# Edge stage of a graph network in ten groups of 500 edges instead of twenty pairs of tiles

## What is computed

```
n    = layernorm(x)
msg  = relu(n[src] + edge_attr @ W_e + b_e)          # 5000 x 512
aggr = segment_sum(msg, dst)                         # 10000 x 512
h    = (1 + eps) * n + aggr
h    = silu(bn(h @ W1 + b1)); h = silu(bn(h @ W2 + b2))
x    = x + h
out  = x + mixture(layernorm(x))                     # 16 experts over groups of 16 tokens
```

## Time and profile before

| | us |
|---|---|
| median of 3 runs | 2110.25 (2109.22 to 2110.86) |
| profiled execution, its time | 2105.35 |
| its span | 2103.6 |
| first stage in it, up to the first DVE instruction of `gnn_up` | 244.1 |
| TensorE granted clock over the span | 0.972 of full |

### The profile page before, as it was taken

The page is one execution under the profiler, slowest core; times in us unless marked ns, Lnnn a source line. Parts: engine busy times, 40 slices in busy tenths (PEclk is TensorE's granted clock), DMA queues, the critical chain, the costliest instruction groups (busy, mean ns, idle before and its releaser), DMA issues. The chain is left out here.

```text
span 2103.6 us, 42031 instructions
## 1 busy us (share of the span) xinstructions
PE 1892.0 (90%) x15720; PEld 1362.7 (65%) x15720; DVE 1194.2 (57%) x2533; ACT 1003.9 (48%) x1742; POOL 386.7 (18%) x481
## 2 busy tenths in 40 slices
PE   0777389999999979999999678999999999999999
PEld 0233178888888858888888565665666666656564
DVE  1457266666566443333333356776766767667666
ACT  0354123333333265565656255565655656556553
POOL 1577230000000000000000141222222222222210
PEclk9998699999999989999999889999999999999999
DMA  9887655666566353343433283343433434334322
GB/s 378 213 156 130 121 154 158 192 181 170 156 190 183 116 183 129 138 154 118 174 117 136 79 288 110 122 131 117 137 117 108 145 108 145 107 117 137 113 75 76
DMA packets 182816, 309.18 MB, mean 147 GB/s; under 512 B 33065, under 2 KB 107305, under 8 KB 179594
## 3 DMA queue, kind: packets, MB, share of 16 engines
q1 hardware_dynamic: 169674, 285.35, 43.5%
q0 software_dynamic: 8960, 20.98, 5.2%
q10 hardware_dynamic: 4032, 0.80, 0.2%
HBM read 172.20 MB, written 134.87 MB: 146 GB/s over the span
## 5 line engine op out<-in xcount | busy, mean ns | idle before, releaser
L1401 PE MATMUL bank<-f2s,inner_bd 128*32 128x512 f32 x2560 | 299.0, 596 | 1.9 <-DVE inner_bd L1012 1.4
L1293 ACT ACTIVATE inter_hi<-bank 128x512 fp32r<-128x512 f32 x320 | 191.1, 597 | 223.1 <-PE bank L1401 221.0
L1226 DVE TENSOR_TENSOR inter_lo<-bank,inter_hi 128x512 fp32r<-128x512 f32 x320 | 220.9, 690 | 100.3 <-ACT inter_hi L1293 98.8
L608 ACT ACTIVATE h1o<-bank,b_by_channel 128x500 f32<-128x500 f32 x160 | 108.5, 678 | 326.7 <-PE bank L423 326.7
L421 PE MATMUL bank<-ahi,w_hi 128*128 128x500 f32 x640 | 250.7, 392 | 14.6 <-DVE alo L762 14.6
L421 PE MATMUL bank<-hhi,w_hi 128*128 128x500 f32 x640 | 251.3, 393 | 2.5 <-DVE hlo L569 2.5
L423 PE MATMUL bank<-hhi,w_lo 128*128 128x500 f32 x640 | 249.6, 390 | 0.0
L422 PE MATMUL bank<-alo,w_hi 128*128 128x500 f32 x640 | 249.2, 389 | 0.0
L422 PE MATMUL bank<-hlo,w_hi 128*128 128x500 f32 x640 | 249.0, 389 | 0.0
L423 PE MATMUL bank<-ahi,w_lo 128*128 128x500 f32 x640 | 248.8, 389 | 0.0
L575 DVE BATCH_NORM_STATS2 stats<-h1o 128x500 f32 (+1 forms) x160 | 103.6, 676 | 162.4 <-ACT h1o L608 162.4
(11 more groups left out here) (124 smaller groups left out, 3182.6 us busy)
## 6 DMA issues: line engine op xcount, KB each, us to landing
h1T<-h1o SPq DMA_DIRECT2D x19, 2000.0 KB, 8.1
h1in<-h1T SPq DMA_DIRECT2D x19, 2000.0 KB, 9.6
aggregate<-zeros SPq DMA_DIRECT2D x20, 1024.0 KB, 8.2
h2in<-h2T SPq DMA_DIRECT2D x40, 512.0 KB, 4.1
x<-in_x SPq DMA_DIRECT2D x80, 256.0 KB, 2.8
x<-x SPq DMA_DIRECT2D x80, 256.0 KB, 3.6
x_back<-x SPq DMA_DIRECT2D x80, 256.0 KB, 3.2
out<-x_back SPq DMA_DIRECT2D x80, 256.0 KB, 2.8
```

Of the source, the lines that this page charges most:

```text
L608: nc.scalar.activation(h1o[b][:, m, :], mb[m % 4][:, 0:CW], ACT.Identity, bias=b1c[:, m:m + 1]).then_inc(evr, 1)
L1226: nc.vector.tensor_tensor(ilo[u % QB][:, :], bI[u % QB][:, :], ihi[u % QB][:, :].bitcast(F32), ALU.subtract).then_inc(ilr, 1)
L1293: nc.scalar.activation(ihi[n % QB][:, :], bI[n % QB][:, :], ACT.Copy).then_inc(ihr, 1)
L1401: last = nc.tensor.matmul(bI[b][32 * i:32 * i + 32, :], ibd[:, e, j, :, :].rearrange("p s g -> p (s g)"), f2s[:, e, :], start=True, stop=True)
```

## The change

The edges are taken as 40 tiles of 125 (partition `p` holds edges `40p` to `40p + 39`), in ten groups ("windows") of four tiles. Sources, destinations and attributes are loaded once, by four DMAs. The row of destinations that `sel` needs comes from PE (`spread`, a transpose of a broadcast column into PSUM) instead of a DMA. In a window, tile `i` is compared with tiles 0 to `i`, so the matrices are 125, 250, 375 and 500 wide, ten 125x125 blocks in all.

The message is no longer normalized by ACT and added by DVE: DVE multiplies by the reciprocal deviation and adds the embedded attributes in one instruction, ACT applies relu with the shift as bias. ACT then copies the message into a rounded high part, DVE subtracts to get a low part, and PE adds up with 20 fp32r products per window (ten blocks, high and low). High and low lie in the buffers of `W2`, free at that time. Four PSUM banks hold embedded attributes; there are 16 row buffers for gathers and 8 for combined rows.

A window's four scatters wait for the four of the window before. Sixteen gathers and three roots are issued before the zeros are waited for. The zeros are made by DVE instead of POOL, and SP issues the loads ahead of them; the rows thrown away are 512 instead of 256. `W1` is loaded once the zeros have landed and split after the last window's `combine`. The hardware loop is gone: all ten windows are written out. The core of the diff, with the lines that only wait or index partly left out:

```diff
-PAIRS = -(-E // (2 * P))
-PU = 4
-ROOTS = 3
+EP, ET = 125, 40
+EW = 4
+EN = ET // EW
+XW = 4
+ZC = 2048
-TRASH = 2 * P
+TRASH = EW * P
...
+        scol, dcol = sb("scol", [P, ET], I32), sb("dcol", [P, ET], I32)
+        ea = sb("ea", [EP, ET, ED])
+        xg = sb("xg", [P, XW * EW, H])
+        sel = [[sb(f"sel{i}_{j}", [P, (j + 1) * EP], F32R) for j in range(EW)] for i in range(3)]
+        comb = sb("comb", [P, 2 * EW, H])
+        mhi, mlo = w2["hi"], w2["lo"]
+        tp, drow, emb, cps = psum[0], psum[1], psum[2:6], psum[6:8]
...
@@ sync
+                sp.wait_ge(const, 2)
+                sp.dma_start(scol[0:EP, :], src.rearrange("(p i) -> p i", i=ET)).then_inc(lds, 16)
+                sp.dma_start(dcol[0:EP, :], dst.rearrange("(p i) -> p i", i=ET)).then_inc(ldd, 16)
+                for p0, p1 in ((0, EP // 16 * 16), (EP // 16 * 16, EP)):
+                    sp.dma_start(ea[p0:p1, :, :], attr[p0:p1]).then_inc(lde, 16)
...
+                sp.wait_ge(zr, 1)
                 for i, (c0, c1) in enumerate(pieces):
...
+                for i in range(ZQ):
+                    sp.wait_ge(zeroed[i], 16 * len(pieces[i::ZQ]))
+                sp.dma_start(w1["whole"][:, :, :], W1.rearrange("(k p) n -> p k n", p=P)).then_inc(w1ld, 16)
@@ scalar
+                def attributes(w):
+                    act.wait_ge(tpr, w + 1)
+                    nc.scalar.activation(eaT[0:ED, w % 2, :], tp[0:ED, 0:EW * EP], ACT.Copy).then_inc(etr, 1)
+                def messages(w):
+                    for t in window(w):
+                        act.wait_ge(prr, t + 1)
+                        nc.scalar.activation(xg[0:EP, s, :], xg[0:EP, s, :], ACT.Relu, bias=nb[0:EP, t:t + 1]).then_inc(msr, 1)
+                        act.wait_ge(msr, t + 1)
+                        nc.scalar.activation(mhi[0:EP, t % (2 * EW), :], xg[0:EP, s, :], ACT.Copy).then_inc(mhr, 1)
+                def collect(w):
+                    if w >= 2:
+                        act.wait_ge(sca, 16 * EW * (w - 1))
+                    for t in window(w):
+                        act.wait_ge(cpr, t + 1)
+                        nc.scalar.activation(comb[0:EP, t % (2 * EW), :], cps[t % 2][0:EP, :], ACT.Copy).then_inc(cbr, 1)
+                for w in range(EN):
+                    if w >= 1:
+                        collect(w - 1)
+                    if w + 1 < EN:
+                        attributes(w + 1)
+                    messages(w)
+                collect(EN - 1)
@@ gpsimd
+                def scatter(w):
+                    pool.wait_ge(ix, w + 1)
+                    if w >= 1:
+                        pool.wait_ge(sca, 16 * EW * w)
+                    for t in window(w):
+                        pool.wait_ge(cbr, t + 1)
                         nc.gpsimd.indirect_dma_start(
...
+                for w in range(XW):
+                    gather(w)
+                for w in range(XW - 1):
+                    root(w)
+                for i in range(ZQ):
+                    pool.wait_ge(zeroed[i], 16 * len(pieces[i::ZQ]))
+                for w in range(EN):
+                    scatter(w)
+                    if w + XW < EN:
+                        gather(w + XW)
+                    if w + XW - 1 < EN:
+                        root(w + XW - 1)
@@ vector
+                nc.vector.memset(zeros[:, :], 0.0).then_inc(zr, 1)
+                nc.vector.memset(comb[:, :, :], 0.0).then_inc(zr, 1)
+                def matches(w):
+                    dve.wait_ge(drp, w + 1)
+                    for t in window(w):
+                        i = t % EW
+                        nc.vector.tensor_scalar(sel[w % 3][i][0:EP, :], drow[0:EP, 0:(i + 1) * EP],
+                                                dcolf[0:EP, t:t + 1], None, ALU.is_equal).then_inc(sl, 1)
...
+                        nc.vector.tensor_tensor_reduce(out=scr[i][0:EP, :], in0=sel[w % 3][i][0:EP, :].bitcast(F32),
...
+                def combine(w):
+                    dve.wait_ge(rst, w + 1)
...
+                    for t in window(w):
+                        dve.wait_ge(emr, t + 1)
+                        nc.vector.scalar_tensor_tensor(out=xg[0:EP, slot(t), :], in0=xg[0:EP, slot(t), :],
+                                                       scalar=rs[0:EP, t:t + 1], in1=emb[t % EW][0:EP, :],
+                                                       op0=ALU.mult, op1=ALU.add).then_inc(prr, 1)
+                    for t in window(w):
+                        dve.wait_ge(mhr, t + 1)
+                        nc.vector.tensor_tensor(mlo[0:EP, t % (2 * EW), :], xg[0:EP, slot(t), :],
+                                                mhi[0:EP, t % (2 * EW), :].bitcast(F32), ALU.subtract).then_inc(mlr, 1)
+                matches(0)
+                matches(1)
+                statistics(0)
+                statistics(1)
+                for w in range(EN):
+                    combine(w)
+                    if w + 2 < EN:
+                        statistics(w + 2)
+                        matches(w + 2)
+                dve.wait_ge(w1ld, 16)
                 for k in range(KH):
                     split_weight(nc.vector, w1["whole"], w1["hi"], w1["lo"], w1h, w1l, k)
@@ tensor
+                def spread(w):
+                    if w >= 1:
+                        pe.wait_ge(sl, EW * w)
+                    for t in window(w):
+                        last = nc.tensor.transpose(drow[0:EP, j * EP:(j + 1) * EP], dcolf[0:EP, t:t + 1].to_broadcast([EP, EP]),
+                                                   ident[0:EP, 0:EP])
+                def add_up(w):
+                    pe.wait_ge(mlr, EW * (w + 1))
+                    for t in window(w):
+                        for i in range(j, EW):
+                            nc.tensor.matmul(cps[t % 2][0:EP, :], pick, mhi[0:EP, s, :], start=(i == j), stop=False)
+                            last = nc.tensor.matmul(cps[t % 2][0:EP, :], pick, mlo[0:EP, s, :], start=False,
+                                                    stop=(i == EW - 1))
+                for w in range(EN):
+                    if w + 2 < EN:
+                        spread(w + 2)
+                    if w + 1 < EN:
+                        turn(w + 1)
+                        embed(w + 1)
+                    add_up(w)
```

More of the change, by code:

```diff
@@ L61, in sb @@
             return ctx.enter_context(nc.sbuf_tensor(name, shape, dt))
-        def buffers(name, shape, dt=F32, n=PU):
-            return [sb(f"{name}{i}", shape, dt) for i in range(n)]
-        zeros = sb("zeros", [P, 2048])
+        zeros = sb("zeros", [P, ZC])
         web = sb("web", [ED + 1, H])
[L68 to L81, removed]
@@ L110, in inputs @@
[L110 to L151, removed]
+        pieces = [(c, min(c + ZC, cols)) for c in range(0, cols, ZC)]
@@ L153, in edge_aggregate, with window, slot @@
+        def window(w):
+            return range(w * EW, (w + 1) * EW)
+        def slot(t):
+            return t % (XW * EW)
         with nc.Block() as block:
@@ L179, in _ @@
-                turns(sp, turn)
+                for i in range(ZQ):
+                    sp.wait_ge(zeroed[i], 16 * len(pieces[i::ZQ]))
+                sp.dma_start(w1["whole"][:, :, :], W1.rearrange("(k p) n -> p k n", p=P)).then_inc(w1ld, 16)
+                with nc.allow_non_contiguous_dma(reason="vectors by channel"):
+                    for name in ("b1", "g1", "beta1", "b2", "g2", "beta2"):
+                        sp.dma_start(vec[name][:, :], vectors[name].rearrange("(m p) -> p m", p=P)).then_inc(vld, 16)
@@ L259, in root @@
-                def root(it, u):
-                    g, u, it = pair_of(it, u)
-                    pool.wait_ge(vpe, g + 1)
-                    nc.gpsimd.tensor_tensor(rs[u][:, :], ve[u][:, :], mhalf[:, :], ALU.pow).then_inc(rst, 1)
-                def scatter(it, u):
-                    g, u, it = pair_of(it, u)
-                    earlier = [(sca, g * 32)] if from_(g, 1) else []
-                    wait_apart(pool, (const, CONST), (cbr, 2 * (g + 1)), *earlier)
-                    for j in range(2):
-                        nc.gpsimd.indirect_dma_start(
-                            out=agg, out_offset=bass.IndirectOffsetOnAxis(ap=idx[u][:, j:j + 1], axis=0),
-                            in_=comb[u][:, j, :], in_offset=None, compute_op=ALU.add).then_inc(sca, 16)
@@ L348, in turn @@
-                def turn(it):
-                    for u in range(PU):
-                        if exists(it, u + 1):
-                            shift(it, u + 1)
-                        add(it, u)
-                        if exists(it, u + 2):
-                            front(it, u + 2)
-                    if isinstance(it, int) and it == TURNS - 2:
-                        dve.wait_ge(w1ld, 16)
-                        for k in range(KH):
-                            split_weight(nc.vector, w1["whole"], w1["hi"], w1["lo"], w1h, w1l, k)
@@ L364, in _ @@
+                matches(0)
[8 more added lines that the diff above has]
```

(15 more changed lines are left out.)

282 lines of the change are left out of this document (107 added, 175 removed).

## The result

| kernel | median us (runs) | ratio to the kernel before | profiled execution | its span | granted clock |
|---|---|---|---|---|---|
| before | 2109.73 (4) | 1 | 2105.35 | 2103.6 | 0.972 |
| changed | 2075.70 (4) | 0.9841 [0.9825, 0.9858] | 2076.01 | 2074.3 | 0.960 |

The change saves 34 us by the medians; 38 us were predicted. The next stage's first VectorE instruction comes at 209.19 us instead of 244.12, 34.9 us earlier; the forecast was 206. The two profiled executions differ by less, 29.3 us, since the stages behind, whose code is the same, took some 5.6 us more in this one profile (2074.3 - 209.2 = 1865.1 us against 2103.6 - 244.1 = 1859.5).

The account below looks back on a forecast made before the run. A chain of POOL writing scatters and waiting for landings bounds the first stage from 68 us, after DMA-bound zeroing. 71 + 129.2 + 2.7 + 2 + 1 = 206 us instead of 244.1, giving 2072 us; range 2059 to 2098.

Parts of the forecast that it names:

- What hides it: Edge loop: DVE and ACT stay hidden beneath POOL, 5 us to spare; window 3 combined from 84.6 us, ninth at 177.
- Scatters in fours: Edge loop: ten landing waits replace twenty; six windows of 13.6 us by POOL's work, four of 11.9 by the chain.
- The start: Before the first scatter: 27.1 MB at 408 GB/s, 66.4 us, from 5 us on, so 71 us.
- `W1`: Its load in window 0 costs 0 to 3.4 us, taken as 2; its split behind the last combining costs 1.
- VectorE: DVE's work per window: statistics 2.96 us, comparisons 4.4, combining paced by ACT 6.9; in all 14.3 us.
- TensorE: PE's work per window: products 4.6 us, embedding and transposes, 10.1 of 13.6 us, hidden at full clock.
- rival 1: PE at its low clock paces the edge loop: windows of 19.2 us, only 18 us saved, 2092 us; chance 0.17.
- Rival 2: Four scatters in flight land more slowly: windows of 16 us, only 7 us saved, 2103 us; chance 0.08.
- Rival 3: DVE's two-input instructions hold up POOL: 8 us slower, 2118 us, chance 0.05; at half price 2095, chance 0.07.
- Rival 4: Nothing saved net: late start at 88 us together with PE pacing at low clock, 2109 us; chance 0.03.

Follow-up runs that it names:

- e1_pairs: Changed kernel, but scatters wait for landings after every two instead of four, gathers split the same way: 2104.76 us, 0.9997 of the kernel before.
- e5_zeros_again: Changed kernel with the first five pieces of zeros written twice, 5.24 MB more: 2087.95 us, stage end 221.09 us.
- e3: Changed kernel with gathers three windows ahead instead of four: 2108.97 us, 1.0001 of the kernel before.
- e4: Changed kernel with the 512 trash rows left unzeroed: 2071.22 us, 0.9833 of the kernel before.
- e8: Changed kernel with gathers three a turn in windows 2 to 5, one root fewer before the zeros, later roots one window later: 2091.50 us, ratio 0.9918.
- e7: Changed kernel with combining moved behind statistics and comparisons of window w + 2 in DVE's order: 2110.36 us, 1.0017 of the kernel before.
- e2: Changed kernel without the messages' low parts, so no such subtractions and half the products: 2066.75 us, 0.9817 of the kernel before.
- e10: Changed kernel with gathers three windows ahead instead of four, issued before the scatters instead of behind: 2073.38 us, 0.9842 of the kernel before.

## Why the prediction was right, and where it was off

The total came out 3.7 us above the forecast and in its range, and the mechanism was the one forecast, but for one step (*What hides it*) that the total didn't show. By its terms, for the profiled execution:

| term | predicted us | measured us |
|---|---|---|
| first scatter | 71 | 73.56 |
| six turns with gathers | 81.6 | 157.02 - 73.56 = 83.5 |
| three turns without | 35.7 | 193.47 - 157.02 = 36.5 |
| last window, barrier, split | 11.9 + 2.7 + 1 = 15.6 | 209.19 - 193.47 = 15.7 |
| `W1`'s load | 2 | in the turns |
| sum | 206 | 209.2 |

*Scatters in fours*: right, 13.91 us in the mean for 13.6 and 12.15 for 11.9, and e1_pairs shows that the landings carry it: all of it by the medians, 29.8 of 34.9 us by the traces. Turns without any stretch are 13.64 us. Of the 1.9 us that the six turns took more than forecast, 0.9 are three scatters of 1.83 to 2.08 us for 1.56 to 1.64, and 0.4 the first turn. POOL waited for a landing before the scatters of the last three windows; I had named four.

*The start*: the bytes and the rate were right (406 GB/s for 408), and e5_zeros_again and the first scatters of e3 and e4 confirm the price of a megabyte. What I missed is the end of it. The share is 1.01 up to 68 us, then 0.99, 0.92, 0.71 and 0.16 in the four microseconds up to 72, so the last pieces don't leave at the full rate; SP, which waits for them, goes on at 72.73 us, and POOL's first scatter starts 0.8 us after that. The slow end and the two delays behind the last byte, for which the sum had nothing, are most of the 2.6 us.

*`W1`*: charged 2 us. The first turn is 14.06 us against 13.64 of the next, 0.4 us; that these are `W1`'s is not shown. Its split was charged 1 us for one stretched scatter; that of 193.47 us took 2.23 us for 1.64, 0.6 us.

*VectorE*: 13.65 us for 14.3. Multiply-and-add takes 2.72 us for four tiles, 0.66 each, where I had 0.64 to 0.68 and twice that as the upper end; relu with a bias and the copy pace the subtractions at 1.27 us (1.25).

*What hides it*: this step failed, and that its cover still held was luck. "Window 3 needs a root that POOL does after scatter 0, so its combining starts at 84.6 us" looked at one of combine(3)'s inputs and not at what stands ahead of it in DVE's queue. Statistics(4) stand there, for rows gathered behind scatter 0, and the combining began at 97.63. Its first tile was copied at 109.81 us (109.21 + 0.60) and written from 114.91:

```profile
109.21 0.60 ACT L160 ACTIVATE comb<-bank 125x512 f32<-125x512 f32 x1 [5.40 <-PE bank L346]
```

So window 3 had 5.1 us in hand. From my own numbers it would have had 27 less about 12 from combining to copy, 15 us. The last window, for which I had 177 us, was combined at 186.8 (186.07 for the last subtraction's start, and 0.69), and 2.2 us were left of 5. e3 (a window less of lead), e8 (a tile and a root late) and e7 (the order) each took what this step had called spare, and lost 15 to 37 us by it.

*TensorE and rival 1*: the premise came true in part. The clock was 0.75 over the loop and not 0.90. TensorE's timeline of the changed kernel, products at both rates:

```profile
107.38 0.63 PE L345 MATMUL bank<-w_hi,sel 125*125 125x512 f32 x1
107.81 0.63 PE L346 MATMUL bank<-w_lo,sel 125*125 125x512 f32 x1
...
109.88 0.40 PE L345 MATMUL bank<-w_hi,sel 125*125 125x512 f32 x1
110.11 0.39 PE L346 MATMUL bank<-w_lo,sel 125*125 125x512 f32 x1
```

Within one window's twenty products they start 0.43 us apart (1.2 GHz) and then 0.23 (2.4 GHz). PE is still busy for only 81 of 134 us, so the window doesn't become the 19.2 us of the rival. e2, at half the products, moved the stage by 1.9 us, which bounds what PE and DVE together take.

*Rival 2*: refuted; four scatters have landed 4.67 to 5.04 us after the last writing, two had in 4.64.

*Rival 3*: refuted in its size, not in its mechanism. A subtraction from 101.30 us lies within the scatter of 101.26, and neither is longer than others (0.69 and 1.64 us); the masked maximum of the prediction lay in the same way. It is otherwise when the subtraction is there first:

```profile
114.78 0.69 DVE L291 TENSOR_TENSOR w_lo<-xg,w_hi 125x512 fp32r<-125x512 f32 x1 [0.59 <-ACT w_hi L152]
114.91 2.08 POOL L212 DMA_INDIRECT aggregate<-comb,idx  x1 [0.20 <-issue]
```

0.56 us were left of the subtraction when this scatter began, and it took 0.44 us more than 1.64. Six scatters of the changed kernel are longer than 1.6 us for 1.55, or than 1.7 for 1.64, and all six began during a subtraction (the last one during one of `W1`'s split), with 0.23 to 0.81 us left of it; each is longer by that less 0.1 to 0.2 us. The rule of the Trainium skill, "SBUF — State Buffer", section "SBUF: two separate sides", by which whichever of the two begins first keeps the other out for a whole instruction, agrees with these rows where DVE began first, and not where the scatter did. The price is small because few scatters begin at such a moment: 1.7 us in all for forty, by e2.

The prediction read the earlier trace rows too narrowly. The scatter of 197.51 us was stretched before the cast of 198.31 us began. What ran when it started was the split's subtraction, with two inputs in SBUF:

```profile
197.17 1.22 DVE L411 TENSOR_TENSOR w_lo<-weight_whole,w_hi 128x1024 fp32r<-128x1024 f32 x1
```

*Rival 4* needed a start at 88 us; it was 73.56.

What stays open: a subtraction that begins 0.04 us after a scatter is not held up, and these rows don't tell why. They give the pattern and e2 its absence (one scatter of e2, of 1.75 us at 174.12, is without a subtraction and unexplained); no run moved the subtractions to test it.

## What to carry to other kernels

When a queue waits for the landing of what it sent, count landings first: here ten fewer were the whole gain by the medians and 29.8 of 34.9 us by the traces, and the other parts were worth little more than that they kept up. To say that a step has time in hand, walk every in-order queue that it stands in and find the latest input of everything ahead of it, not of the step alone; then test the lead by taking one buffer away. When two engines slow each other down, look at which instruction was running when the slow one began, not at what ran beside it later. A wait's named releaser has to be compared with the end of that instruction before it is believed.

## What the runs showed that I had not expected

Issuing gathers ahead of the scatters and not behind them was as good as a fourth window of buffers (0.9842 against 0.9841), although the gathers then delay each scatter by their 5 us: POOL's sum of work is the same. With one window less of lead and the old order, turns alternated between 14 and 21 to 24 us, instead of growing evenly, since behind each late window the next one's rows had arrived (combine(3) of e3 followed at 108.87 us without a wait). The four-column root on POOL takes 1.05 us, for 0.74 with two columns, as estimated. Where it stands directly behind a scatter, as in e10 (80.31 us) or at 163.67 us in the changed kernel, its row is 1.6 us long and begins some 0.55 us before the scatter's ends; in e10 DVE was idle then, so DVE is not the reason.
